# Two transposes moved behind the down matmuls, and three weight tiles put elsewhere in SBUF, in a grouped mixture-of-experts stage

## The chip, the cores and the metric

The kernel runs on one core of one Trainium2 chip. The metric is the device time of one execution in microseconds, the median over several executions.

## The reference

The model is one layer with two halves. The first is a state-space mixer over x of shape (4, 1024, 256) with its own layer norms. The second, on which the change bears, is a mixture of experts with 8 experts of which each token takes 2, and a shared expert:

```python
xn = (xf - mu) * rsqrt(var + eps) * ln_gamma + ln_beta          # 4096 tokens x 256
probs = softmax(xn @ router_w);  topv, topi = top_k(probs, 2)   # weights made to sum to 1
for e in range(8):                                              # gate_up (256, 2048), down (1024, 256)
    gate, up = split(xn @ gate_up_w[e])
    out += comb[:, e] * (silu(clip(gate, -10, 10)) * up) @ down_w[e]
out += swiglu(xn, shared_gate_up_w, shared_down_w)
x = x + layernorm(out)
```

## The kernel before

The mixer, the router and the shared expert take the first part of the span, with an order of work written out by hand for each engine (the dictionary ORDER). Nothing of that is changed. While they run, the expert weights are split into a high and a low part and stored in HBM (w_split), and each token's normed row is scattered to HBM (xs_scratch) so that the rows of one expert stand together.

The expert stage then takes 39 groups (NG) of 256 token rows (G), each group for one expert. A group is one call of turn(g, par), the same in form on every engine, where par is g modulo 2 and picks one of two buffers. A turn has 8 chunks (FC, the loop over f), each of 128 of the expert's 1024 hidden channels:

- gate_up(g, par, f) on TensorE: 12 matmuls of 256 columns, with the weights of the chunk (w_gu[f]) as stationary operand and the group's transposed rows (xg_hi and xg_lo, 256 columns) as moving operand. A product is made of three: high by high, high by low, low by high (L1354 to L1356). They fill gu_ps[f % 2]. Before them TensorE waits for the chunk's weights (loaded[f]) and for VectorE to have emptied that bank (h_ready, of chunk f - 2).
- VectorE clips the gate (L1464), ScalarE takes the silu (L1414), VectorE multiplies by up (L1471), ScalarE writes the high part (L1406) and VectorE the low part (L1459, h_lo_ready).
- down(g, par, f) on TensorE: 6 matmuls of 256 columns (L1365 to L1367), with the hidden values as stationary and the chunk's down weights (w_d[f], high and low) as moving operand. It runs LAG = 3 chunks later: behind gate_up(g, f) come the down matmuls of chunk f - 3, for f below 3 those of chunk 5 + f of the group before.
- turn_rows(g + 1, ..., c) on TensorE: two 128x128 transposes (L1342) of the next group's rows (half c of their 256 columns) into x_ps, one pair at f = 1 and one at f = 4. The first waits for the rows' load (rows_loaded). ScalarE reads them out (L1397 and L1400) behind its silu of chunk 2 and of chunk 5.

TensorE carries out its instructions in the order in which the loop writes them:

```python
gate_up(g, par, f)
if f in (1, 4):
    turn_rows(g + 1, 1 - par, (f - 1) // 3)
if f >= LAG:
    down(g, par, f - LAG)
elif not (isinstance(g, int) and g == 0):
    down(g - 1, 1 - par, FC + f - LAG)
```

The queue of SyncE issues the loads. load_chunk(g, f) waits until down has used chunk f's old weights (down_done), then loads gate-up and down weights (L1239 and L1240), in fact only when the expert changes (cond=new). After chunk 1 it loads the rows of the group after (L1227), which waits for x_turned, the count of transposed halves. Before the first groups, L450 writes blank rows behind each expert's rows (xs_scratch<-pad).

All tiles of the expert stage lie in buffers of the mixer, as float32 columns of a partition. Gate-up weights of chunks 0 to 5 are in w_both, of chunk 6 in xs_hi and of chunk 7 in xs_lo, each from column 0. The down weights (d_ring) stand behind them: chunks 0 and 2 to 5 in w_both with an offset of D_AT = 48 columns, chunk 7 in xs_lo with the same offset, chunk 6 in xs_hi with offset 0, and chunk 1 in h_hi[0], behind the rows of even groups. The transposed rows (x_home) start at column X_AT = 48 of h_hi, the hidden values (h_home) at column 0 of h_lo.

Of the kernel before, what the change touches and what calls it, by code (L numbers as in the profile page):

```python
# [13 lines left out]
B, L, D, H = 4, 1024, 256, 512  # L14
# [3 lines left out]
HALF = 512  # L18
# [27 lines left out]
G = 256  # L46
# [7 lines left out]
SPARE = E * CAP  # L54
WB = E * FC // B
WS = 3
X_AT, D_AT, R_AT = 48, 48, 0
GUW = 2 * 4 * P
XS = 5

# [1 line left out]
def mixer(nc, x, w_e, w_s, weights, full, consts, shared, xs_dram, x1_dram, acc_dram, fill, vec, ident,  # L62
# [3 lines left out]
    with ExitStack() as ctx:  # L66
        def sb(name, shape, dt=F32):
            return ctx.enter_context(nc.sbuf_tensor(name, shape, dt))
# [7 lines left out]
        h_hi = [sb(f"h_hi{i}", [P, HC, HALF], F32R) for i in range(2)]  # L76
        h_lo = [sb(f"h_lo{i}", [P, HC, HALF], F32R) for i in range(2)]
# [11 lines left out]
        g = sb("g", [P, DC, HALF])  # L89
# [119 lines left out]
        flat = lambda v: v.rearrange("p a b -> p (a b)")  # L209
        quad = lambda v: v.rearrange("p (a b c) -> p a b c", a=2, b=2)  # L210
        xs_flat = [flat(v[:, :, :]) for v in (xs_hi, xs_lo)]
        d_base = (FC - 2) * GUW + D_AT
        gu_ring = [w_both[:, f * GUW:(f + 1) * GUW] for f in range(FC - 2)] + [v[:, 0:GUW] for v in xs_flat]
        d_ring = [w_both[:, d_base + f * 2 * D:d_base + (f + 1) * 2 * D] for f in range(FC - 2)]
        d_ring += [v[:, GUW + at:GUW + at + 2 * D] for v, at in zip(xs_flat, (0, D_AT))]
        d_ring[1] = flat(h_hi[0][:, :, :])[:, GUW + HALF // 8:GUW + HALF // 8 + 2 * D]
        u_flat, cv_flat, x_flat = flat(u[:, :, :]), flat(cv[:, :, :]), flat(x_in[:, :, :])
        x_home = [flat(v[:, :, :])[:, X_AT:X_AT + 2 * DC * G] for v in h_hi]
        h_home = [flat(v[:, :, :])[:, 0:4 * G] for v in h_lo]
        by_tile = lambda v: v.rearrange("p (t d) -> p t d", d=D)  # L220
        acc = [by_tile(flat(xnt[:, k, :, :])) for k in range(XS)] + [by_tile(x_flat[:, k * TC * D:(k + 1) * TC * D]) for k in range(2)]
        acc += [by_tile(flat(s[:, :, :]))]
# [956 lines left out]
def experts(nc, ctx, w_s, xs_dram, acc_dram, x1_dram, out, group_expert, group_change, group_row, group_code, vec, ident, neg_half,  # L1179
# [153 lines left out]
    def tensor(pe):  # L1333
        def turn_rows(g, par, c):

            if c == 0:
                pe.wait_ge(rows_loaded[par], (g_half(g, par)) * 16 + 16)
                if isinstance(g, int) and g == 0:
                    free(pe, "x_ps")
            pe.wait_ge(x_f_ready, g * DC + c + 1)  # L1340
            for t in range(GT):
                i = nc.tensor.transpose(x_ps[:, t * P:(t + 1) * P], rows[:, par, t, c * P:(c + 1) * P], ident[:, :])  # L1342
            i.then_inc(x_turned, 1)

        def gate_up(g, par, f):
            pe.wait_ge(loaded[f], 32 if isinstance(g, int) and g == 0 else g * 32)
            if f == 0:
                pe.wait_ge(x_lo_ready, g * DC + DC)
            pe.wait_ge(h_ready, g * FC + f + 1)
            for m, at in enumerate((0, 2 * P)):  # L1350
                out = gu_ps[f % 2][:, m * G:(m + 1) * G]
                for c in range(DC):
                    cols = slice(at + c * P, at + (c + 1) * P)
                    nc.tensor.matmul(out, gu_hi[f][:, cols], xg_hi[:, par, c, :], start=c == 0, stop=False)  # L1354
                    nc.tensor.matmul(out, gu_hi[f][:, cols], xg_lo[:, par, c, :], start=False, stop=False)  # L1355
                    i = nc.tensor.matmul(out, gu_lo[f][:, cols], xg_hi[:, par, c, :], start=False, stop=c == DC - 1)  # L1356
            i.then_inc(gu_done, 1)
        def down(g, par, f):
            pe.wait_ge(h_lo_ready, g * FC + f + 1)
            if f == 0:  # L1360
                pe.wait_ge(y_ready, g + 1)
            for t in range(GT):
                toks = slice(t * P, (t + 1) * P)
                out = down_ps[par][t][:, 0:D]
                nc.tensor.matmul(out, hg_hi[:, f % 4, toks], d_hi[f], start=f == 0, stop=False)  # L1365
                nc.tensor.matmul(out, hg_hi[:, f % 4, toks], d_lo[f], start=False, stop=False)  # L1366
                i = nc.tensor.matmul(out, hg_lo[:, f % 4, toks], d_hi[f], start=False, stop=f == FC - 1)  # L1367
            i.then_inc(down_done, 1)

        def turn(g, par):  # L1370
            for f in range(FC):
                gate_up(g, par, f)
                if f in (1, 4):
                    turn_rows(g + 1, 1 - par, (f - 1) // 3)
                if f >= LAG:
                    down(g, par, f - LAG)
                elif not (isinstance(g, int) and g == 0):
                    down(g - 1, 1 - par, FC + f - LAG)

        def first_turn(b, c):  # L1380
            turn_rows(0, 0, c)

        def rest():
            free(pe, "gu_ps")
            turn(0, 0)
            free(pe, "down_ps")
            with pe.Fori(0, (NG - 1) // 2) as i:
                for k in range(2):
                    turn(i * 2 + 1 + k, 1 - k)
            for f in range(FC - LAG, FC):  # L1390
                down(NG - 1, (NG - 1) % 2, f)
        return first_turn, rest
# [41 lines left out]
    def vector(dve):  # L1434
# [82 lines left out]
        return seeds, first_lo, rest  # L1517

    return sync, gpsimd, tensor, scalar, vector


def g_half(g, par):

    if isinstance(g, int):
        return g // 2
    return (g - par) // 2


def program(nc, d, out):
    scratch = lambda name, shape: nc.dram_tensor(name, shape, F32, kind="Internal").ap()  # L1530
    x1_dram = scratch("x1_scratch", (B, L, D))
    xs_dram = scratch("xs_scratch", (SPARE + G, ROW))
    acc_dram = scratch("acc_scratch", (T + G, D))
    w_s = scratch("w_split", (E, FC, P, 2 * CW))
    with ExitStack() as ctx:
        def sb(name, shape, dt=F32):
            return ctx.enter_context(nc.sbuf_tensor(name, shape, dt))

        vec = sb("vec", [P, V_COLS])
        group_expert = sb("group_expert", [P, NG + 1], I32)  # L1540
        group_change = sb("group_change", [P, NG + 1], I32)
        group_row = sb("group_row", [P, NG + 1], I32)
        group_code = sb("group_code", [P, NG + 1])
        zeros = sb("zeros", [P, GT * D])
        tok_id = sb("tok_id", [P, TT], I32)
        pad = sb("pad", [P, GT, ROW])
        tables = [sb("start_row", [P, E]), sb("limits", [P, E, MAXG]), sb("group_no", [P, NG + 1, E]), sb("number", [P, NG + 1])]
        fill = sb("fill", [P, E])
        ident = sb("ident", [P, P])
        neg_half = sb("neg_half", [P, LT])  # L1550
        mixer(nc, d["x"], d["w_e"], w_s,
              [(DL_AT, d["dl_w_t"], DC), (A_AT, d["A_w_t"], DC), (B_AT, d["B_w_t"], DC), (C_AT, d["C_w_t"], HC),
               (DD_AT, d["D_w_t"], DC)],
              [(W1_AT, d["w1_t"], DC), (W2_AT, d["w2_t"], DC), (W3_AT, d["w3_t"], DC), (RT_AT, d["router"], DC)],
              d["vecs"], [(SGU_AT, d["sgu"], DC), (SDN_AT, d["sdn"], SC)], xs_dram, x1_dram, acc_dram,
              fill, vec, ident, tok_id, pad, zeros, neg_half, tables,
              group_expert, group_change, group_row, group_code, out)
# [24 lines left out]
```

## Time and profile before

| what | value |
|---|---|
| median of 3 executions | 1183.02 us (1178.42 to 1184.69) |
| the profiled execution, its own time | 1178.42 us |
| its span, first to last instruction | 1176.3 us |
| TensorE busy (matmuls) | 1082.7 us, 92% of the span |
| weight loads / VectorE / ScalarE / GpSimd busy | 961.2 / 833.1 / 655.2 / 302.2 us |
| mean granted TensorE clock | 0.973 |

Busy times are shares of the span. A matmul's recorded duration holds its way through the array and so overlaps the next one's; how fast matmuls follow each other is read from their starts. "Idle before" is the time in which an engine did nothing ahead of an instruction, and the name behind it is what ended that time.

### The profile page before, as it was taken

To read this page: it belongs to the slowest core of one execution; us is meant where nothing else is said; L and a number is where in the kernel's file an instruction comes from. 1 tells how busy PE (TensorE), PEld (TensorE's weight loads), DVE (VectorE), ACT (ScalarE), POOL (GpSimd) and SP (SyncE) were. 2 spreads that over 40 slices of the span, in tenths; PEclk is the share of its full clock that TensorE was granted. 3 is DMA by queue.
4 is the path that set the end of the run, shared out by engine and by line. 5 is a ranking of instruction groups with operands and counts; after the bars stand their busy time and mean duration, and the time that the engine had idled before them with its cause. 6 is when DMAs were issued, how large, how long until landed. Compare 5 with 4: busy or idle time off the path is not lost.

```text
span 1176.3 us, 24227 instructions
## 1 busy us (share of the span) xinstructions
PE 1082.7 (92%) x7492; PEld 961.2 (82%) x7492; DVE 833.1 (71%) x2113; ACT 655.2 (56%) x1325; POOL 302.2 (26%) x358
## 2 busy tenths in 40 slices
PE   4889999899979998899999999999999999999940
PEld 2665776677757666899999999999999999999940
DVE  5996899898877766566666666666666666666645
ACT  6778867778574364444544454544445444545425
POOL 1142032733441534012211221122122212211225
PEclk9999999999998999999999999999999999999985
DMA  8654776974663789523321236746922268212239
GB/s 304 208 213 172 251 231 210 318 240 145 223 229 140 247 284 320 195 59 64 72 56 35 36 86 210 222 130 192 379 67 36 60 208 250 36 19 35 36 81 222
DMA packets 122219, 191.72 MB, mean 163 GB/s; under 512 B 9792, under 2 KB 76864, under 8 KB 122176
## 3 DMA queue, kind: packets, MB, share of 16 engines
q1 hardware_dynamic: 105760, 170.38, 42.7%
q0 software_dynamic: 16416, 20.85, 10.5%
q8 instruction: 17, 0.28, 0.1%
q14 instruction: 26, 0.21, 0.1%
HBM read 295.62 MB, written 86.41 MB: 325 GB/s over the span
## 4 chain that ended last, share of the span: by engine, by line
PE 75%; DVE 8%; issue 4%; DMA 4%; POOL 3%; SPq 3%; ACT 3%; another core or an unknown queue 0%; ACTq 0%; DVEq 0%; POOLq 0%
PE bank L1354 11%; PE bank L1356 11%; PE bank L1355 11%; PE bank L470 10%; PE bank L1365 6%; PE bank L1367 6%; PE bank L1366 6%; PE bank L464 4%; PE bank L465 3%; PE bank L466 3%; POOL xs_scratch L1150 2%; PE bank L1342 1%; DMA w_both<-w_split 1%; DVE h L902 1%; DVE xr L1495 1%
## 5 line engine op out<-in xcount | busy, mean ns | idle before, releaser
L1304 POOL DMA_INDIRECT acc_scratch<-cv,ids x78 | 124.3, 1594 | 548.5 <-DVE cv L1443 508.4
L1464 DVE TENSOR_SCALAR cv<-bank 128x256 f32<-128x256 f32 x312 | 132.3, 424 | 185.3 <-PE bank L1356 185.3
L1354 PE MATMUL bank<-h_hi,w_both 128*128 128x256 f32 x936 | 260.3, 278 | 1.7 <-DVE cv L1471 1.2
L1355 PE MATMUL bank<-h_hi,w_both 128*128 128x256 f32 x936 | 259.6, 277 | 0.0
L1356 PE MATMUL bank<-h_hi,w_both 128*128 128x256 f32 x936 | 259.6, 277 | 0.0
L1414 ACT ACTIVATE cv<-cv 128x256 f32<-128x256 f32 x312 | 130.5, 418 | 225.5 <-DVE cv L1464 224.7
L1406 ACT ACTIVATE h_lo<-cv 128x256 fp32r<-128x256 f32 x312 | 130.0, 417 | 114.9 <-DVE cv L1471 113.4
L1354 PEld LDWEIGHTS bank<-h_hi,w_both 128*128 128x128 f32 x936 | 176.5, 189 | 3.1 <-issue 2.1
L1356 PEld LDWEIGHTS bank<-h_hi,w_both 128*128 128x128 f32 x936 | 176.4, 188 | 0.0
L1355 PEld LDWEIGHTS bank<-h_hi,w_both 128*128 128x128 f32 x936 | 176.4, 188 | 0.0
L1471 DVE TENSOR_TENSOR cv<-bank,cv 128x256 f32<-128x256 f32 x312 | 132.6, 425 | 47.6 <-ACT cv L1414 43.9
L1459 DVE TENSOR_TENSOR h_lo<-cv,h_lo 128x256 fp32r<-128x256 f32 x312 | 129.7, 416 | 0.8 <-ACT h_lo L1406 0.6
L464 PE MATMUL bank<-xs_hi,w_both 128*128 128x512 f32 x224 | 99.8, 445 | 22.3 <-DVE delta L852 9.1
L1365 PE MATMUL bank<-w_both,h_lo 128*128 128x256 f32 x390 | 107.7, 276 | 0.0
L1366 PE MATMUL bank<-w_both,h_lo 128*128 128x256 f32 x390 | 107.7, 276 | 0.0
L1367 PE MATMUL bank<-w_both,h_lo 128*128 128x256 f32 x390 | 107.7, 276 | 0.0
L466 PE MATMUL bank<-xs_hi,w_both 128*128 128x512 f32 x224 | 90.0, 402 | 0.0
L465 PE MATMUL bank<-xs_lo,w_both 128*128 128x512 f32 x224 | 89.8, 401 | 0.0
L1150 POOL DMA_INDIRECT xs_scratch<-n,slot_now x64 | 69.6, 1087 | 62.1 <-DVE slot_now L990 33.0
L464 PEld LDWEIGHTS bank<-xs_hi,w_both 128*128 128x128 f32 x224 | 43.9, 196 | 40.2 <-issue 14.6
L1133 POOL TENSOR_TENSOR h_lo<-h,h_hi 128x512 fp32r<-128x512 f32 x32 | 49.0, 1535 | 106.2 <-ACT h_hi L724 106.0
L1365 PEld LDWEIGHTS bank<-w_both,h_lo 128*128 128x128 f32 x390 | 73.2, 188 | 0.0
(233 smaller groups left out, 2558.2 us busy)
## 6 DMA issues: line engine op xcount, KB each, us to landing
w_both<-w_split SPq DMA_DIRECT2D x228, 512.0 KB
w_both<-w_split SPq DMA_DIRECT2D x190, 256.0 KB
e_raw<-w_e SPq DMA_DIRECT2D x64, 384.0 KB
w_split<-e_high SPq DMA_DIRECT2D x64, 384.0 KB
w_split<-e_raw SPq DMA_DIRECT2D x64, 384.0 KB
xs_hi<-w_split SPq DMA_DIRECT2D x38, 512.0 KB
xs_lo<-w_split SPq DMA_DIRECT2D x38, 512.0 KB
u<-xs_scratch SPq DMA_DIRECT2D x40, 260.0 KB, 3.2
```

The lines of the kernel that those rows point to most:

```text
L464: nc.tensor.matmul(out, hi, x_hi, start=first, stop=False)
L1354: nc.tensor.matmul(out, gu_hi[f][:, cols], xg_hi[:, par, c, :], start=c == 0, stop=False)
L1355: nc.tensor.matmul(out, gu_hi[f][:, cols], xg_lo[:, par, c, :], start=False, stop=False)
L1356: i = nc.tensor.matmul(out, gu_lo[f][:, cols], xg_hi[:, par, c, :], start=False, stop=c == DC - 1)
L1365: nc.tensor.matmul(out, hg_hi[:, f % 4, toks], d_hi[f], start=f == 0, stop=False)
L1366: nc.tensor.matmul(out, hg_hi[:, f % 4, toks], d_lo[f], start=False, stop=False)
L1367: i = nc.tensor.matmul(out, hg_lo[:, f % 4, toks], d_hi[f], start=False, stop=f == FC - 1)
L1406: nc.scalar.activation(hg_hi[:, f % 4, :], gate[:, f % 4, :], ACT.Copy).then_inc(h_hi_ready, 1)
L1414: nc.scalar.activation(gate[:, f % 4, :], gate[:, f % 4, :], ACT.Silu).then_inc(silu_ready, 1)
L1459: nc.vector.tensor_tensor(hg_lo[:, f % 4, :], gate[:, f % 4, :], hg_hi[:, f % 4, :], ALU.subtract).then_inc(h_lo_ready, 1)
L1464: nc.vector.tensor_scalar(gate[:, f % 4, :], gu_ps[f % 2][:, 0:G], CLIP, -CLIP, ALU.min, ALU.max).then_inc(clipped, 1)
L1471: nc.vector.tensor_tensor(gate[:, f % 4, :], gu_ps[f % 2][:, G:2 * G], gate[:, f % 4, :], ALU.mult).then_inc(h_ready, 1)
```

## The change

Three edits.

1. In TensorE's loop the pair of transposes stands behind the down matmuls of its turn instead of ahead of them. With f = 1 and 4 the order gate_up(f), transposes, down, gate_up(f + 1) becomes gate_up(f), down, transposes, gate_up(f + 1). In the first group there is no down at f = 1, so that pair stays where it was.
2. The down weights of chunk 1 go from h_hi[0] to their regular place in w_both, and those of chunk 6 in xs_hi from offset 0 to offset 48.
3. The offset of the hidden values gets a name, H_AT = 0, with the value that it had.

```diff
-X_AT, D_AT, R_AT = 48, 48, 0
+X_AT, H_AT, D_AT, R_AT = 48, 0, 48, 0
...
         d_ring = [w_both[:, d_base + f * 2 * D:d_base + (f + 1) * 2 * D] for f in range(FC - 2)]
-        d_ring += [v[:, GUW + at:GUW + at + 2 * D] for v, at in zip(xs_flat, (0, D_AT))]
-        d_ring[1] = flat(h_hi[0][:, :, :])[:, GUW + HALF // 8:GUW + HALF // 8 + 2 * D]
+        d_ring += [v[:, GUW + D_AT:GUW + D_AT + 2 * D] for v in xs_flat]
...
-        h_home = [flat(v[:, :, :])[:, 0:4 * G] for v in h_lo]
+        h_home = [flat(v[:, :, :])[:, H_AT:H_AT + 4 * G] for v in h_lo]
...
         def turn(g, par):
             for f in range(FC):
                 gate_up(g, par, f)
-                if f in (1, 4):
-                    turn_rows(g + 1, 1 - par, (f - 1) // 3)
                 if f >= LAG:
                     down(g, par, f - LAG)
                 elif not (isinstance(g, int) and g == 0):
                     down(g - 1, 1 - par, FC + f - LAG)
+                if f in (1, 4):
+                    turn_rows(g + 1, 1 - par, (f - 1) // 3)
```

## Rows read from the trace of the kernel before

**Rows 1.** The page, part 4: the chain that ended last, by line.
```profile
PE bank L1354 11%; PE bank L1356 11%; PE bank L1355 11%; PE bank L470 10%; PE bank L1365 6%; PE bank L1367 6%; PE bank L1366 6%; PE bank L464 4%; PE bank L465 3%; PE bank L466 3%; POOL xs_scratch L1150 2%; PE bank L1342 1%; DMA w_both<-w_split 1%; DVE h L902 1%; DVE xr L1495 1%
```
**Rows 2.** Windows (PE, PEld, DVE, ACT, POOL busy us (count), PEclk, DMA share, GB/s).
```profile
492.00:1132.00 640.00, 638.56 (x5588) 637.18 (x5587) 421.82 (x1172) 313.34 (x756) 121.21 (x76) 1.00 0.39 106
```
**Rows 3.** Waits of TensorE from 464 to 1140 us: total, times, longest.
```profile
PE bank L1342 <- DMA u<-xs_scratch: 3.6, 1, 3.6
PE bank L1354 <- DVE cv L1471: 1.2, 2, 0.7
```
**Rows 4.** Timeline of TensorE, a chunk without transposes: its first matmul and the next chunk's.
```profile
603.91 0.28 PE L1354 MATMUL bank<-h_hi,w_both 128*128 128x256 f32 x1
...
605.95 0.28 PE L1354 MATMUL bank<-h_hi,w_both 128*128 128x256 f32 x1
```
**Rows 5.** Timeline of TensorE around a pair of transposes, then down and gate-up.
```profile
607.20 0.28 PE L1356 MATMUL bank<-h_hi,w_both 128*128 128x256 f32 x1
607.32 0.38 PE L1342 MATMUL bank<-ident,u 128*128 128x128 f32 x2
607.46 0.36 PE L1365 MATMUL bank<-xs_hi,h_lo 128*128 128x256 f32 x1
607.66 0.28 PE L1366 MATMUL bank<-xs_hi,h_lo 128*128 128x256 f32 x1
...
609.17 0.28 PE L1356 MATMUL bank<-h_hi,w_both 128*128 128x256 f32 x1
...
609.51 0.28 PE L1356 MATMUL bank<-h_hi,w_both 128*128 128x256 f32 x1
```
**Rows 6.** Timeline of the weight loads of the same pair and of what follows.
```profile
607.22 0.24 PEld L1342 LDWEIGHTS bank<-ident,u 128*128 128x128 f32 x2
607.43 0.19 PEld L1365 LDWEIGHTS bank<-xs_hi,h_lo 128*128 128x128 f32 x1
```
**Rows 7.** Timeline of TensorE in group 0, gate-up of chunk 2 right behind the transposes.
```profile
468.51 0.36 PE L1354 MATMUL bank<-h_hi,w_both 128*128 128x256 f32 x1 [0.49 <-DVE cv L1471]
468.70 0.28 PE L1355 MATMUL bank<-h_hi,w_both 128*128 128x256 f32 x1
...
470.19 0.28 PE L1356 MATMUL bank<-h_hi,w_both 128*128 128x256 f32 x1
```
**Rows 8.** Timeline of TensorE behind a short stall, up to the next transposes.
```profile
982.14 0.28 PE L1355 MATMUL bank<-h_hi,w_both 128*128 128x256 f32 x1
...
987.56 0.28 PE L1356 MATMUL bank<-h_hi,w_both 128*128 128x256 f32 x1
```
**Rows 9.** Line L1365 by form: count, duration in ns min/median/max, first and last start.
```profile
L1365 PE MATMUL bank<-w_both,h_lo x390: 276/276/281, 471.3 to 1130.0; 128*128 128x256 f32 x195
...
L1365 PE MATMUL bank<-h_hi,h_lo x78: 282/322/365, 473.5 to 1123.2; 128*128 128x256 f32 x78
...
L1365 PE MATMUL bank<-xs_hi,h_lo x78: 280/282/365, 487.8 to 1130.7; 128*128 128x256 f32 x78
```
**Rows 10.** Timeline of TensorE at the one long idle time of the stage.
```profile
487.62 0.43 PE L1342 MATMUL bank<-ident,u 128*128 128x128 f32 x2 [3.63 <-DMA u<-xs_scratch]
```
**Rows 11.** The chain that ended last, what led up to that transpose.
```profile
479.69 4.36 DMA xs_scratch<-pad
...
484.78 2.72 DMA u<-xs_scratch
```
**Rows 12.** Windows as in rows 2: idle times of TensorE and what followed them.
```profile
61.06:63.26 2.20, 0.00 (x1) 0.01 (x1) 2.20 (x3) 1.22 (x3) 2.09 (x2) 1.00 0.56 172
63.26:66.70 3.44, 3.44 (x15) 2.82 (x16) 3.41 (x6) 1.02 (x2) 0.71 (x2) 1.00 0.58 233
...
488.41:491.82 3.41, 3.41 (x19) 3.41 (x18) 0.26 (x1) 0.00 (x0) 0.00 (x0) 0.50 0.05 17
```
**Rows 13.** Timeline of VectorE in the turns of rows 5.
```profile
603.77 0.42 DVE L1459 TENSOR_TENSOR h_lo<-cv,h_lo 128x256 fp32r<-128x256 f32 x1
```
**Rows 14.** Timeline of ScalarE in the turn of rows 5.
```profile
610.61 0.55 ACT L1397 ACTIVATE h_hi<-bank,vec 128x256 fp32r<-128x256 f32 x1
```

## Prediction

> **What bounds the kernel now.** I read the chain that ended last first [rows 1]. The six matmul lines of the expert stage (L1354 to L1356, L1365 to L1367) hold 51% of the span, more than anything else, and the transposes (L1342) 1%. The windows come next [rows 2]: from 492 to 1132 us matmuls are recorded for 638.56 of 640 us at full clock, VectorE for 422 and ScalarE for 313. So in this stage TensorE sets the end, and a change in it counts one to one. The list of TensorE's waits says the same from the other side: in the whole stage it waits once for long, 3.6 us for a load of rows, and otherwise for about 1 us in all on VectorE [rows 3].
>
> A busy TensorE can still be a slow one, so the starts in the timeline have to be read. A chunk without transposes is 18 matmuls (12 gate-up, 6 down) in 605.95 - 603.91 = 2.04 us, 113.3 ns each [rows 4]. A chunk with a pair of transposes takes 609.51 - 607.20 = 2.31 us for the same 18 [rows 5]. So a pair costs 0.27 us, and there are two in each of 39 groups: 21 us of the kernel. The change rearranges what stands around them.
>
> **What of a pair's cost can move.** The two weight loads of the pair start at 607.22, the next one at 607.43 [rows 6]. That is 0.105 us each, close to the 0.113 us of a full matmul, and stays in either order, since each transpose needs its load: 0.21 of the 0.27 us. The other 0.06 us lies in the handover. From the first down matmul behind the pair to the second it takes 607.66 - 607.46 = 0.20 us, and the 13 intervals after that take 609.17 - 607.66 = 1.51 us against 13 x 113.3 = 1.473, that is 0.037 us too much [rows 5]. What can be won at the 76 ordinary pairs is therefore at most about 0.05 us each, 4 us in all.
>
> **Edit 1, the order.** After the change a pair is followed by gate-up of chunk 2 or 5. The old kernel shows that succession once: in group 0 there is no down at f = 1, and gate-up of chunk 2 stands right behind the transposes [rows 7]. There the first interval is 468.70 - 468.51 = 0.19 us, and the 13 after it 470.19 - 468.70 = 1.49 us, 0.017 too much. Against rows 5 this is 0.01 + 0.02 = 0.03 us less. TensorE had stalled 0.49 us just before, so the specimen isn't pure. It is the nearest row, and I take it. Pairs that change their place: 38 at f = 1 (groups 1 to 38) and 39 at f = 4, of which one is counted apart below. 76 x 0.03 = -2.3 us. The ends are 76 x 0.05 = -4 us (no loss left) and, on the other side, the slow pace of the first rival.
>
> What the six down matmuls need is there early. The low part of the hidden values of chunk 6 is written from 603.77, done 0.42 us later, and the first matmul that reads it starts at 607.46 [rows 5, 13]; starting 0.23 us sooner costs nothing with 3.3 us of slack. If that cover were gone, the loss would be at most these 0.23 us a pair, 18 us, but nothing in the stage's waits points to it: down waits for VectorE nowhere in these rows [rows 3]. The transposes come later by six matmuls, 0.68 us. Their first reader is ScalarE at 610.61, behind its silu of chunk 2 [rows 14]; the pair would end near 608.4 instead of 607.7. Slack 2.2 us, cost nothing. The rows' buffer is handed back to SyncE 0.7 us later, but the queue gets to that wait only behind the loads of chunk 1, which wait for down of chunk 1, and that now comes 0.23 us earlier. Only at the few changes of expert is there anything to transfer. I cost this at nothing, with 0.3 us either way.
>
> **The one long wait.** In turn 1 the pair waits for its rows for 3.63 us, up to 487.62 [rows 10]. What led up to it is SyncE's own: blank rows written, landed at 484.05, then the load, landed at 487.50 [rows 11]. None of it depends on TensorE, so the moment of 487.6 stays. The down matmuls of chunk 6, now behind the transposes, will be done within the wait: -0.7 us (6 x 0.118). The wait is then about 2.9 us. It was followed by 3.41 us at a granted clock of 0.50, the 1.2 GHz level, in which 19 matmuls are counted, those at its edges among them [rows 12]. At that level a 256-column matmul lasts at least 256 / 1.2 GHz = 0.213 us, so 16 fit in whole; at 0.113 us they would take 1.8 us. The fall cost 1.6 us. An idle time of 2.20 us was not followed by a fall: the clock stayed at 1.00 [rows 12]. 2.9 us lies half way between the two. I take it that the clock still falls, because the part of the wait that is left is the same one, ending at the same moment: nothing here, and -1.6 us as the other end.
>
> **Edit 2, the places.** Down matmuls that read their moving operand from w_both take 276 ns in the median (least 276), those from h_hi 322 (least 282) and from xs_hi 282 (least 280) [rows 9]. It would be tempting to book the difference to the places: 6 ns and more times 6 matmuls times two chunks times 39. But these two chunks are just the ones that follow the transposes, which explains the same durations, and the excess is already in the 0.037 us above. Behind no transposes, a matmul on these places should run like the others on w_both and xs_lo. Zero, and no more than what is left of the 4 us bound. Each load keeps its size and count, and in w_both it waits for nothing new. **Edit 3** changes no address: zero.
>
> **The sum.** 1178.4 - 0.7 - 2.3 = 1175.4 us for the profiled execution, 0.25% below its own time. That execution was the fastest of three, 4.6 us under their median, and I put the same shift on the median: 1180.0 us. A difference of 0.5% (5.9 us) is about what a measurement of this kernel can tell from none, and the three executions spread over 6.3 us themselves.
>
> **Rivals.**
>
> *Slower: the pace that doesn't come back.* TensorE has a second pace. Behind a short stall at 981.9 the next 46 intervals take 987.56 - 982.14 = 5.42 us, 117.8 ns each [rows 8], with no wait between and through gate-up and down matmuls alike; only the next transposes ended it. Usually the slow pace dies out within some ten matmuls, as in rows 5, but the old kernel shows that for transposes followed by down. If it holds behind transposes followed by gate-up, each matmul until the next pair costs 4.5 ns more: 54 matmuls after f = 1, 90 after f = 4. Over 38 groups that is 9.2 us, 15.4 us or, for both, 24.6 us, giving for the median 1189, 1196 or 1205. It would be decided at the handover, and it becomes slower by over 0.5% from about 2000 matmuls in the slow pace (5.9 + 3.0 us over 4.5 ns), of 5616. For it: the specimen of rows 8 lies right there, at gate-up of chunk 2, and edit 2 changes the addresses that are read together. Against it: rows 7, where gate-up of chunk 2 behind transposes recovered. Behind the pair at f = 4 the old kernel has no specimen at all.
>
> *Nothing but the wait.* The excess belongs to the transposes and whatever follows them, and only the 0.7 us stay: 1182.3. For it: the first interval is nearly the same, 0.19 and 0.20. By a rule of the Trainium skill ("TensorE: Matmul & The Clock Gate", section "Step-by-step: what each phase is for") TensorE reads the moving operand and the next weights through two independent ports, so that where the tiles lie should matter to neither. By that rule the sum of edit 2 is zero, as above, and the slow pace could not come from the places; no row here tells whether it does.
>
> *Faster: the clock doesn't fall.* At a wait of 2.9 us the clock may stay up, and the handover may lose all its 0.05 us: -0.7 - 1.6 - 4 = -6.3 us, 1176.7.
>
> **Chances.** Forecast 0.50; slow pace 0.24, nearly all of it above 0.5%; nothing but the wait 0.14; the clock kept, with or without the whole handover, 0.12. Faster by over 0.5% needs nearly every gain at once, or luck in the spread: 0.12. Slower 0.22, the same 0.66. Range: down to 1173 (1176.7 and the spread of executions) and up to 1198, which takes in the slow pace behind one of the two pairs but not behind both. The likeliest case alone gives 1176 to 1184.
>
> **What the new profile would show.** In a chunk with transposes the order of lines is 1356, 1365 to 1367, 1342, 1354. The chunk of 18 matmuls with a pair takes 2.28 us (2.31 now), the others stay at 2.04. If the slow pace holds, they take 2.12 over whole stretches. The wait before the transposes in turn 1 is 2.9 us, with the same end as now. A row of granted clock 0.50 behind it says whether the clock fell. The waits of TensorE get no new entry; an entry of down for VectorE's low part, or of ScalarE for the transposes, would mean that I have misread the slack. I would be wrong most plainly if many chunks took 2.12 us, or if TensorE got new waits for weights at changes of expert.

## The result and the profile after

Over 9 executions the changed kernel takes 1189.57 us in the median (1185.15 to 1198.64), the kernel before 1180.00 us (1176.92 to 1186.13, 9 executions). The ratio is 1.0064 with a 95% interval from 1.0039 to 1.009: slower by 0.6%. By that ratio it is 7.6 us, by the two medians 9.6 us. I had forecast 0.25% faster. The time lies in the range I gave, but the sign is that of my first rival, which I had given 0.24.

The profiled execution of the changed kernel was a lucky one: 1178.98 us, below all nine others. That of the kernel before, 1178.42 us, was its third fastest. So the two spans alone (1176.9 and 1176.3 us) show nothing. Inside them the stage tells the difference. The windows view of the changed kernel over the same 640 us as in [rows 2] (columns as there):

```profile
492.00:1132.00 640.00, 638.91 (x5520) 637.73 (x5520) 416.25 (x1155) 308.76 (x746) 119.76 (x75) 1.00 0.39 106
```

TensorE is as busy and as fully clocked as before, and yet 5520 matmuls stand here against 5588. No records are missing: in both traces the matmuls between one pair of transposes and the next are complete (54 or 90, as below). Busy time can't show this loss; the count in a window does. 68 matmuls at 115 ns are 7.8 us.

The timeline of TensorE, only the transposes of the changed kernel (each row is a pair; lines have moved up by one, so L1341 was L1342):

```profile
568.20 0.38 PE L1341 MATMUL bank<-ident,u 128*128 128x128 f32 x2
574.56 0.38 PE L1341 MATMUL bank<-ident,u 128*128 128x128 f32 x2
585.00 0.38 PE L1341 MATMUL bank<-ident,u 128*128 128x128 f32 x2
591.58 0.38 PE L1341 MATMUL bank<-ident,u 128*128 128x128 f32 x2
602.41 0.38 PE L1341 MATMUL bank<-ident,u 128*128 128x128 f32 x2
```

and the same of the kernel before:

```profile
613.71 0.38 PE L1342 MATMUL bank<-ident,u 128*128 128x128 f32 x2
624.19 0.38 PE L1342 MATMUL bank<-ident,u 128*128 128x128 f32 x2
630.58 0.38 PE L1342 MATMUL bank<-ident,u 128*128 128x128 f32 x2
```

Between a pair at f = 1 and the next at f = 4 lie 54 matmuls, between that and the next f = 1 another 90; I call them the short and the long stretch. Before, they took 6.39 us (630.58 - 624.19) and 10.48 us. Now the first turn shows 6.36 and 10.44 us, and the next 6.58 and 10.83 us. Inside the slow short stretch the timeline reads:

```profile
588.75 0.28 PE L1364 MATMUL bank<-w_both,h_lo 128*128 128x256 f32 x1
...
590.87 0.28 PE L1364 MATMUL bank<-w_both,h_lo 128*128 128x256 f32 x1
```

A chunk of 18 matmuls in 2.12 us, 117.8 ns each, against 2.04 us in [rows 4]. That is the pace of [rows 8].

To count it I took the starts of all matmuls of the stage, and called a stretch slow when its mean interval, the first 14 and the last left out, was above 116 ns. There are 38 stretches of each kind. Before: 2 short and 1 long slow. Only one of these three, at 981 us [rows 8], has the slow pace; the other two have a high mean from a wait or from the low clock behind [rows 10]. After: 17 short and 19 long, all in the slow pace. I call an interval of 116 to 121 ns a slow one: 559 before, 2635 after. The 2076 more, at 4.5 ns, are 9.3 us. That is a rough figure, since the matmuls with both tiles at column 0 (below) count as slow too.

The waits of TensorE in the stage of the changed kernel (total, times, longest):

```profile
PE bank L1341 <- DMA u<-xs_scratch: 0.9, 1, 0.9
PE bank L1353 <- DMA w_both<-w_split: 0.8, 3, 0.4
PE bank L1364 <- DVE h_lo L1458: 0.3, 1, 0.3
```

The long wait for rows fell from 3.6 us [rows 3] to 0.9 us, more than the 0.7 us of the change. What released it, in the chain that ended last:

```profile
474.40 4.17 DMA xs_scratch<-pad
...
479.30 2.70 DMA u<-xs_scratch
```

Both come 5.3 to 5.5 us earlier than in [rows 11], and the mixer, which the change doesn't touch, ended 2.9 us earlier. That is the spread between executions. And the clock stayed at 1.00 afterwards, in the windows from that transpose on:

```profile
482.13:485.50 3.37, 3.37 (x30) 3.37 (x31) 1.36 (x5) 1.29 (x4) 0.00 (x0) 1.00 0.26 91
```

So the lucky execution gained 2.9 us in the mixer, 2.7 us of wait (0.7 us of it by the change) and 1.6 us of clock, 7.2 us in all. The stage lost 7.8 us, and 0.6 us is left, the difference of the two spans. The loss is real also in an execution whose time doesn't show it.

### The profile page after: what moved, and what is told of

Read it like the earlier page. It is cut to its first block, busy times and chain, and to the rows that moved or that the text cites. A ratio compares the mean times of both kernels' runs of the same rounds, so it can differ in the third digit from the quotient of the medians.

```text
span 1176.9 us, 24227 instructions
## 1 busy us (share of the span) xinstructions
PE 1089.7 (93%) x7492; PEld 968.4 (82%) x7492; DVE 834.7 (71%) x2113; ACT 655.1 (56%) x1325; POOL 303.2 (26%) x358
## 4 chain that ended last, share of the span: by engine, by line
PE 78%; DVE 6%; DMA 4%; SPq 4%; issue 3%; ACT 3%; POOL 2%; ACTq 0%; DVEq 0%; POOLq 0%
PE bank L469 13%; PE bank L1353 11%; PE bank L1354 11%; PE bank L1355 11%; PE bank L1364 6%; PE bank L1366 6%; PE bank L1365 6%; PE bank L463 4%; PE bank L464 4%; PE bank L465 4%; DMA w_both<-w_split 2%; PE bank L1341 1%; POOL xs_scratch L1149 1%; DVE xr L1494 1%; PE bank L480 1%
## 5 line engine op out<-in xcount | busy, mean ns | idle before, releaser
L1353 PE MATMUL bank<-h_hi,w_both 128*128 128x256 f32 x936 | 267.7, 286 | 0.8 <-DMA w_both<-w_split 0.8
L1354 PE MATMUL bank<-h_hi,w_both 128*128 128x256 f32 x936 | 260.8, 279 | 0.0
L1355 PE MATMUL bank<-h_hi,w_both 128*128 128x256 f32 x936 | 260.6, 278 | 0.0
L1366 PE MATMUL bank<-w_both,h_lo 128*128 128x256 f32 x468 | 130.4, 279 | 0.0
L1364 PE MATMUL bank<-w_both,h_lo 128*128 128x256 f32 x468 | 130.3, 278 | 0.0
L1365 PE MATMUL bank<-w_both,h_lo 128*128 128x256 f32 x468 | 130.3, 278 | 0.0
L1366 PEld LDWEIGHTS bank<-w_both,h_lo 128*128 128x128 f32 x468 | 88.4, 189 | 0.0
L1364 PEld LDWEIGHTS bank<-w_both,h_lo 128*128 128x128 f32 x468 | 88.2, 188 | 0.0
L1365 PEld LDWEIGHTS bank<-w_both,h_lo 128*128 128x128 f32 x468 | 87.9, 188 | 0.0
```

## The experiments

Twelve kernels. Those with a ratio were timed over several executions beside the kernel before. The others ran once, and of them I use the trace, not the time. Their times show why: chunk 6 alone took 1179.47 us, chunk 1 in w_both 1175.40, chunk 7 at 0 1181.66 and gate-up 5 shifted 1188.21 us, but the one execution of the kernel before beside them took 1165.86 us, 11 us less than the fastest of its nine above. The kernel with the hidden values shifted took 1189.74 us, beside a median of 1181.88. First the two halves of the change apart.

**The order alone**, down weights at their old places:

```diff
 gate_up(g, par, f)
-if f in (1, 4):
-    turn_rows(g + 1, 1 - par, (f - 1) // 3)
 if f >= LAG:
     down(g, par, f - LAG)
 ...
+if f in (1, 4):
+    turn_rows(g + 1, 1 - par, (f - 1) // 3)
```

> The transposes behind down, but the down weights of chunks 1 and 6 at their old places. Theory A (what follows the transposes decides: behind gate-up the slow pace of 117.8 ns holds): as the changed kernel, about half of the 76 stretches behind transposes slow, over 2000 intervals in the slow pace, 0.4 to 0.9% over the kernel before. Theory B (the places decide, the order is inert): the slow pace in no more than a few stretches, no more than 600 intervals, and the time within 0.3% of the kernel before, or 1 to 3 us below it for the shorter handover.

Measured: ratio 1.0096 (1.006 to 1.0131), median 1195.32 us; 19 short and 35 long stretches slow, 4220 slow intervals. The median is higher than that of the whole change, though the two intervals of the ratio overlap; what is clear is that the order alone already costs 0.6% or more. Theory B falls.

**The places alone**, transposes ahead of down:

```diff
-d_ring += [v[:, GUW + at:GUW + at + 2 * D] for v, at in zip(xs_flat, (0, D_AT))]
-d_ring[1] = flat(h_hi[0][:, :, :])[:, GUW + HALF // 8:GUW + HALF // 8 + 2 * D]
+d_ring += [v[:, GUW + D_AT:GUW + D_AT + 2 * D] for v in xs_flat]
```

> The transposes ahead of down as before, but the down weights of chunks 1 and 6 at their new places. Theory A: behind down the pace comes back, at most 600 slow intervals, the time within 0.3% of the kernel before. Theory B (the old places are what brought the pace back behind the transposes): slow stretches as many as in the changed kernel or more, up to all 76 (5600 intervals, +25 us, 2%).

Measured: ratio 1.0068 (1.0043 to 1.0092), median 1190.71 us; 17 short and 18 long stretches slow, 2488 slow intervals. Theory A, which was the one in my prediction, falls too: transposes followed by down lose the pace as well. Neither half is harmless and the losses don't add up. The stretches at 113.3 ns here tell one thing more:

```profile
575.99 0.39 PE L1341 MATMUL bank<-ident,u 128*128 128x128 f32 x2
582.36 0.38 PE L1341 MATMUL bank<-ident,u 128*128 128x128 f32 x2
592.79 0.38 PE L1341 MATMUL bank<-ident,u 128*128 128x128 f32 x2
```

They take 6.37 and 10.43 us, the same as such stretches of the changed kernel, though down still follows the transposes. In the run with the order alone such stretches take 6.38 to 6.39 and 10.46 us, nearly as before. So the 0.03 us that a fast handover of the changed kernel saves come with the places and not with the order. The kernel before needs both things at once: transposes followed by down, and those two chunks at the old places. What do the old places have in common? In xs_hi chunk 6 starts at column 1024, in h_hi chunk 1 at 1024 + 64. Both are 0 modulo 64, as is the start of every stationary tile of the 256-column matmuls; all their other moving tiles start at 48 modulo 64. That is theory C.

**Chunk 6 alone to offset 48**, else the kernel before:

```diff
-d_ring += [... for v, at in zip(xs_flat, (0, D_AT))]
+d_ring += [... for v, at in zip(xs_flat, (D_AT, D_AT))]
```

> The kernel before, with the down weights of chunk 6 alone moved to offset 48. Theory C (in the old kernel the first matmuls behind a pair read a tile that starts at the same column modulo 64 as their stationary operand; such matmuls run slower themselves and thereby end the slow pace): the stretches behind the pair at f = 1 are slow in about half of the groups, those at f = 4, where chunk 1 still lies at its old place, all recover. Theory D (any other arrangement breaks the luck): slow stretches behind both pairs.

Measured: 18 of 38 short stretches slow, 1 of 38 long ones. Its pairs in the timeline:

```profile
588.56 0.38 PE L1342 MATMUL bank<-ident,u 128*128 128x128 f32 x2
595.14 0.38 PE L1342 MATMUL bank<-ident,u 128*128 128x128 f32 x2
605.61 0.38 PE L1342 MATMUL bank<-ident,u 128*128 128x128 f32 x2
```

6.58 us for the short stretch, behind which chunk 6 no longer restores the pace, and 10.47 us for the long one, where chunk 1 still does. As theory C had it; D falls.

**Chunk 1 in w_both, at a column that is 0 modulo 64**:

```diff
-d_ring[1] = flat(h_hi[0][:, :, :])[:, GUW + HALF // 8:GUW + HALF // 8 + 2 * D]
+d_ring[0] = d_ring[1]
+d_ring[1] = w_both[:, d_base - D_AT:d_base - D_AT + 2 * D]
```

> The kernel before, with the down weights of chunk 1 in w_both, but at a column that is 0 modulo 64 (the first slot, at offset 0; chunk 0 takes the slot of chunk 1). Theory C: nearly all stretches recover at f = 1 and at f = 4, as in the kernel before. Theory E (chunk 1 has to be outside w_both): the stretches behind the pair at f = 4 slow in about half of the groups.

Measured: 3 short and 1 long stretch slow, 623 slow intervals. Here the column makes the difference and not the buffer.

**Down of chunk 7 at offset 0**, in the changed kernel:

```diff
-d_ring += [v[:, GUW + D_AT:GUW + D_AT + 2 * D] for v in xs_flat]
+d_ring += [v[:, GUW + at:GUW + at + 2 * D] for v, at in zip(xs_flat, (D_AT, 0))]
```

> The changed kernel, with the down weights of chunk 7 at offset 0 instead of 48; these down matmuls come 12 gate-up matmuls behind the pair at f = 1. Theory C: a slow stretch behind that pair ends there, so that it lasts 12 to 18 matmuls and not 54, and where the pace is 113 ns the six matmuls take about 6 ns more each. Theory F (only what stands directly behind the transposes counts): slow stretches at f = 1 last their full length in about half of the groups.

Measured: no short stretch of the 38 slow in its full length; 20 of 38 long ones as before. In the timeline of TensorE, from a pair on:

```profile
554.52 0.28 PE L1354 MATMUL bank<-h_hi,w_both 128*128 128x256 f32 x1
...
555.81 0.28 PE L1364 MATMUL bank<-xs_lo,h_lo 128*128 128x256 f32 x1
...
556.52 0.29 PE L1353 MATMUL bank<-h_hi,w_both 128*128 128x256 f32 x1
...
556.88 0.28 PE L1353 MATMUL bank<-h_hi,w_both 128*128 128x256 f32 x1
...
557.90 0.28 PE L1364 MATMUL bank<-w_both,h_lo 128*128 128x256 f32 x1
```

Eleven intervals in 1.29 us, 117 ns each: slow. Then down 7: six in 0.71 us, 118 ns. Then gate-up: three in 0.36 us, and the nine after them in 1.02 us, 113.3 ns. The pace is back behind these six in all 38 short stretches, and it didn't have to be restored right behind the transposes. Theory F falls.

**Gate-up 5 shifted by 48 columns**, in the changed kernel, so that its two operands start at the same column:

```diff
+gu_ring[5] = w_both[:, 5 * GUW + D_AT:6 * GUW + D_AT]
```

> The changed kernel, with the gate-up weights of chunk 5 shifted by 48 columns, so that stationary and moving operand of gate-up 5 start at the same column modulo 64. Theory C: the stretches behind the pair at f = 4 (followed by gate-up 5) all recover, with intervals of 120 to 124 ns among the first ones, and those at f = 1 stay slow in about half of the groups. Theory A' (only down can bring the pace back): f = 4 stays slow in about half.

Measured: the opposite. All 38 long stretches slow, 31 short ones, 5029 slow intervals.

```profile
557.85 0.28 PE L1355 MATMUL bank<-h_hi,w_both 128*128 128x256 f32 x1
...
558.81 0.28 PE L1365 MATMUL bank<-w_both,h_lo 128*128 128x256 f32 x1
...
559.51 0.28 PE L1354 MATMUL bank<-h_hi,xs_hi 128*128 128x256 f32 x1
```

Eight intervals in 0.96 us: 120 ns among the shifted matmuls, as theory C said. But behind them six in 0.70 us, 117 ns, and it goes on so. Half of theory C stands (same start column, 120 ns), the other half (and thereby the pace comes back) fails here.

**Hidden values of chunks 1 and 5 shifted by 48 columns**, old order, new places, to see whether it is gate-up or the shift:

```diff
-h_home = [flat(v[:, :, :])[:, H_AT:H_AT + 4 * G] for v in h_lo]
+h_slots = [[flat(v[:, :, :])[:, at:at + G] for at in (0, 4 * G + D_AT, 2 * G, 3 * G)] for v in h_lo]
```

> Transposes ahead of down as in the kernel before, down weights at the new places, and the hidden values of chunks 1 and 5 shifted by 48 columns, so that both operands of down 1 (behind the pair at f = 4) and of down 5 start at column 48 modulo 64. Theory C1 (the same start column of both operands in down is enough): f = 4 stretches all recover. Theory C2 (the moving operand has to start at 0, or the stationary one must not be shifted): f = 4 stretches slow in half of the groups or in all, as with the shifted gate-up 5.

Measured: 22 long stretches slow in full, and 28 short ones, in which nothing differs from the run of the places alone (17 slow there); they follow down 5 and gate-up 1. In the other 16 long ones the matmuls are fast until down 5, and slow behind it:

```profile
552.97 0.28 PE L1353 MATMUL bank<-h_hi,w_both 128*128 128x256 f32 x1
...
553.30 0.28 PE L1364 MATMUL bank<-w_both,h_lo 128*128 128x256 f32 x1
...
554.02 0.28 PE L1353 MATMUL bank<-h_hi,w_both 128*128 128x256 f32 x1
...
555.32 0.28 PE L1355 MATMUL bank<-h_hi,w_both 128*128 128x256 f32 x1
```

Three intervals in 0.33 us (110, the two decimals of the view), six of down 5 in 0.72 us, eleven in 1.30 us (118 ns). Behind down 5, with both tiles at 48, all 38 long stretches are slow, the 16 that were fast until then among them; behind down 7, with both at 0, all were fast. But it also depends on where they stand: down 1, with both tiles at 48 and directly behind the transposes, was followed by the fast pace in those same 16. C2 holds, and why the two columns differ stays open.

**Down of chunks 2 and 7 at 0**, in the changed kernel, to see whether the pace is the whole loss:

```diff
+d_ring[2] = w_both[:, d_base - D_AT:d_base - D_AT + 2 * D]
+d_ring[0] = w_both[:, d_base + 2 * 2 * D:d_base + 3 * 2 * D]
-d_ring += [v[:, GUW + D_AT:GUW + D_AT + 2 * D] for v in xs_flat]
+d_ring += [v[:, GUW + at:GUW + at + 2 * D] for v, at in zip(xs_flat, (D_AT, 0))]
```

> The changed kernel, with the down weights of chunks 7 and 2 at a column that is 0 modulo 64 (chunk 0 takes chunk 2's slot). Their down matmuls come 12 gate-up matmuls behind the pair at f = 1 and at f = 4. Theory C (the slow pace is the whole loss): no stretch slow beyond these 12, some 600 to 1000 slow intervals in all, the time within 0.3% of the kernel before. Rival (the order itself costs something beside the pace): still 0.4% or more over it.

Measured: ratio 1.0014 (0.9991 to 1.0038), median 1182.99 us against 1181.88; 1 short and 1 long stretch slow in full, 1284 slow intervals, more than the 600 to 1000 I expected; the 725 beyond the 559 of the kernel before are 3.3 us at 4.5 ns, or 0.3%. With the new order in place and the pace restored, no loss can be told from zero any more; up to 0.38% isn't excluded. The rival, 0.4% or more from the order itself, falls.

**Both pairs together at f = 1**, old order, chunk 6 at offset 0 and chunk 1 at its regular place (this line and the use of the other half of x_ps are left out of the cut), which by theory C should beat both kernels:

```diff
-if f in (1, 4):
-    turn_rows(g + 1, 1 - par, (f - 1) // 3)
+if f == 1:
+    for c in range(DC):
+        turn_rows(g + 1, 1 - par, c)
```

> The kernel before, with both pairs of transposes together at f = 1, into two halves of the same bank, and chunk 1 at its regular place. One handover a group instead of two: by theory C 0.05 us less for each of 38 groups, 2 us, -0.2%, with hardly any slow stretch. Rival: the four transposes cost the same as two pairs, 0.0%.

Measured: ratio 1.000 (0.998 to 1.002). In the timeline:

```profile
595.09 0.60 PE L1342 MATMUL bank<-ident,u 128*128 128x128 f32 x4
611.90 0.60 PE L1342 MATMUL bank<-ident,u 128*128 128x128 f32 x4
```

A turn takes 16.81 us against 16.87 (624.19 in the rows above - 607.32 in [rows 5]): 0.06 us less, where I expected 0.05, and 2.3 us over 38 turns. But 5 of the 38 turns are in the slow pace throughout, and 926 intervals are slow against 559 in the kernel before: 1.7 us at 4.5 ns. What is left, 0.6 us or 0.05%, is far below what this ratio can tell. Four of these turns begin with a short idle time of TensorE, such as this one, where 0.25 us lie between the starts of the last down matmul and of gate-up instead of 0.12 (the fifth is the first of all, in group 0, where no down follows the transposes):

```profile
713.83 0.28 PE L1367 MATMUL bank<-xs_hi,h_lo 128*128 128x256 f32 x1
714.08 0.38 PE L1354 MATMUL bank<-h_hi,w_both 128*128 128x256 f32 x1
```

It stands behind six matmuls with both tiles at 0, and the slow pace followed all the same and lasted to the end of the turn. So those six matmuls restore the pace, but it can be lost again at the next idle time, and with one such chunk in a turn instead of two a lost pace stays lost longer.

**Other distances** than 48 columns: 32 in the kernel before; 40 and 56 with the old order and the new places.

```diff
-X_AT, D_AT, R_AT = 48, 48, 0
+X_AT, D_AT, R_AT = 32, 32, 0
```

> The kernel before with the distance between the operands' start columns 32 instead of 48 (X_AT and D_AT). Theory G (the steady pace hangs on this distance): another steady pace than 113.3 ns. Theory H (it is a pace of the weight loads alone): 113.3 ns, and the slow stretches few as before or about half.

> The kernel with the new places and the old order (in which 35 of 76 stretches were slow), with 40 columns instead of 48 between the operands' start columns. Theory G (the distance modulo 64 sets how the pace settles): another share of slow stretches, between that of 48 and the steady 119 ns of 32, so most or all of them slow, 1195 to 1205 us. Rival: 48 is nothing special, about half slow, near 1190 us.

> As the run with 40 columns, with 56. Theory G: a share of slow stretches other than half; if 113.3 ns needs room before the operands meet again at distance 0 (64), more than with 48; if it needs only distance from 32, fewer or none, which would give a kernel at or below the one before, 1165 to 1183 us. Rival: about half slow.

Measured in one execution each: 1204.75 us for 32 (the kernel before, on the same chip, 1181.88 in the median), 1191.95 and 1198.23 us for 40 and 56 (the kernel before 1173.89 in one execution); 1191.95 is below the 1195 to 1205 I expected. In all three every one of the 76 stretches is slow. The windows view with distance 32, then that of the kernel before over the same time:

```profile
490.00:1130.00 640.00, 639.15 (x5374) 638.55 (x5373) 404.54 (x1126) 300.30 (x725) 119.60 (x72) 1.00 0.40 104
```

```profile
490.00:1130.00 640.00, 638.84 (x5585) 637.66 (x5584) 421.41 (x1171) 312.86 (x755) 121.21 (x76) 1.00 0.39 106
```

4% fewer matmuls for the same busy time. The intervals go round between 115 and 124 ns there, 118 to 119 in the mean. Of the five distances tried (0, 32, 40, 48, 56), only 48 gave 113.3 ns. H falls.

## Why the prediction was wrong

The step that failed is that of edit 1: that a pair followed by gate-up behaves like [rows 7]. I took one specimen, behind a stall of 0.49 us, for 76 handovers. In 40 of them the fast pace came back: they took 0.03 us less than before (6.36 against 6.39, 10.44 against 10.48 us). That is the size I gave, but by luck: the places alone give the same 6.36 and 10.43 us and the order alone 0.02 us at most, so I had compared gate-up at column 48 with down at column 0 and put the difference down to the order. In 36 the slow pace stayed. They took 0.19 us more in the short stretch (6.58) and 0.35 us in the long one (10.83): 17 x 0.19 + 19 x 0.35 - 40 x 0.03 = 8.7 us. Less 0.7 us of the wait that is 8.0 us, and 7.6 us (9.6 by the medians) were measured.

- The first rival named the mechanism and the price (4.5 ns a matmul, 54 and 90 matmuls), and 2000 matmuls as the point from which it decides; there were 2076. Its price for a stretch was a little high, 0.24 and 0.40 us against the 0.19 and 0.35 measured. It had all stretches of a kind slow or none; about half of each were. I weighed it too low: that the slow pace lasts until something ends it stood in [rows 8], and I had no row that showed what ends it.
- Edit 2 was costed at zero because places were not to matter. They do: alone, edit 2 makes the kernel 0.7% slower. The durations of [rows 9] held a trace of it that I explained away by the transposes ahead. The runs part the two. The first two lines are down of chunk 7, twelve matmuls behind the transposes, at column 48 (the changed kernel) and at 0; the third is the places alone, down of chunk 6 at column 48 and right behind the transposes:

```profile
L1364 PE MATMUL bank<-xs_lo,h_lo x78: 276/276/385, 483.8 to 1131.9; 128*128 128x256 f32 x78
L1364 PE MATMUL bank<-xs_lo,h_lo x78: 277/282/386, 487.9 to 1134.6; 128*128 128x256 f32 x78
L1364 PE MATMUL bank<-xs_hi,h_lo x78: 276/323/561, 488.3 to 1138.9; 128*128 128x256 f32 x78
```

  So the 322 ns were of the transposes, as I said, but 282 against 276 is what column 0 makes of a down matmul without transposes right ahead. These are the matmuls with both tiles at 0, 116 to 121 ns apart, and they are what restored the pace.
- The rival "nothing but the wait", with the rule of the Trainium skill beside it that moving operand and next weights come through two independent ports ("TensorE: Matmul & The Clock Gate", section "Step-by-step: what each phase is for"), fell. As I had used it, that rule left nothing for the start column to change; the page itself says nothing of start columns. Here a distance of 32 columns instead of 48 cost 4% of the stage's matmuls, so for the pace of weight load and matmul together the measurement decides against reading it so. Whether the ports or something else is what meets, no run here tells.
- The slack was right: no wait on ScalarE, and the waits for weights stayed below 1 us. The one wait of down for VectorE's low part, 0.3 us in the list above, is in the kernel before too, where I had said that there was none:

```profile
PE bank L1365 <- DVE h_lo L1459: 0.3, 1, 0.3
```

- The long wait: its end hangs on SyncE alone, as I said, but that end moves by several us between executions. In fourteen profiles the idle time there was 0.9 to 4.1 us. The clock fell behind it in six: always at 3.0 us or more (4 times), never below 2.2 us, and in between it fell at 2.27 and 2.49 us and not at 2.30 and 2.46 us. My 0.7 us and the clock's 1.6 us are inside that spread.

What stays open: why a handover ends in the one pace or the other. In the changed kernel it follows a fixed pattern over long rows of groups, the long stretches for instance fast and slow in turn, so it is not chance. I read it as a matter of phase between weight load and matmul, but no experiment isolated the phase. Open too is why the order alone makes 35 long stretches slow and the whole change only 19.

## What to carry to other kernels

When TensorE is busy all the time, count its matmuls in a window or read their start-to-start times; a kernel can lose 4% there that no busy share and no wait shows. A stream of weight loads and matmuls can settle into more than one steady pace. Which paces there are, and what brings the fast one back, depended here on the start columns of the two tiles that are read together, modulo 64 float32 columns: treat a place in SBUF that looks arbitrary as part of the timing, and measure before tidying it. A single specimen of a succession, taken behind a stall, does not show what 76 of them will do.

## What the runs showed of the hardware that I had not expected

For pairs of a 128x128 weight load and a 256-column float32r matmul at full clock: 113.3 or 117.8 ns apart when the moving tile starts 48 columns (192 bytes) beyond the stationary one modulo 64, and the second, once entered, lasted over whole stretches of 54 and 90. 118 to 120 ns when both start at the same column. Between 115 and 124 ns in a repeating pattern when they start 32, 40 or 56 apart.

Six matmuls with both tiles at 0, twelve matmuls behind the transposes, brought 113.3 ns back in 38 of 38 cases (down 7). Directly behind the transposes, in the kernel before, with chunk 1 in w_both and with both pairs together, they did too, but for eight cases (1, 3 and 4), each with an idle time of TensorE ahead of the gate-up that follows; with the clock at its lower level during them one stretch of the run with chunks 2 and 7 stayed slow. Matmuls with both tiles at 48 ended in 117.8 ns in 38 of 38 cases behind gate-up 5 (twelve) and behind down 5 (six), but down 1, six of them directly behind the transposes, in only 22 of 38.
